# A mixture-of-experts kernel on one core: the last token block made, scaled and scattered in two halves of its channels

## The chip, the cores and the metric

The kernel runs on one core of one Trainium2 chip. The metric is the device time of one execution in microseconds (us), given as the median of several executions; lower is better. Engine names in the rows: PE is TensorE (matmuls), PEld is its weight load, DVE is VectorE, ACT is ScalarE, POOL is GpSimd, SP is SyncE, which issues most plain DMAs. The indirect DMAs, which gather or scatter rows by a list of row numbers, are issued by POOL.

## What is computed

The input x has 8 x 256 tokens of 512 channels in f32. A first layer adds a gated recurrent mix to x (an exponentially decaying average over time of a context, weighted by exp of the normalised x). A second layer adds a gated mixture of experts, and it is in this layer that the change lies:

```
logits = flat_x @ Wg + bg                       # 2048 tokens, 4 experts
top_vals, top_idx = top_k(logits, 2)            # each token picks 2 experts
for i in range(4):                              # experts
    sel_p, sel_idx = top_k(score_i, 512)        # each expert keeps its 512 best tokens
    tok = flat_x[sel_idx]                       # 512 x 512
    h = gelu(tok @ W1[i])                       # 512 x 2048
    y = h @ W2[i] * p                           # 512 x 512, one factor for each token
    out = out.at[sel_idx].add(y)
x = x + tanh(g_ffn) * out
```

## The kernel before

The first part of the program (about the first 130 us) computes the recurrent layer, stores x1 to the result tensor in HBM, stores its normalised rows to a table in HBM, and picks each expert's 512 tokens. Then the four experts follow one another. For an expert, POOL gathers the 512 token rows from the table in four blocks of 128, PE turns them over, and they are split into a high and a low f16 half, as are both weight matrices. A product in near-f32 precision is three f16 matmuls: high by high, high by low, low by high.

`up_product` makes h for one expert: 16 slices of 128 hidden units, each 12 matmuls with 512 tokens in the moving operand. ACT applies the gelu (line 954), DVE splits h in `halves_of_h_and_w2` (lines 1528 to 1533).

`down_block(e, s)` makes the output rows of token block s (128 tokens, of which an expert has ST = 4) for expert e: for each of HT = 16 slices of hidden units it loads the 128 tokens of h as the stationary operand and streams the 512 channels of W2, three times for the three halves, so 48 matmuls of 128x512. They accumulate in one PSUM bank, `PY[s % 2]`, bank 2 or 3. When it is done, PE raises `c_y`. DVE's `take_y(e, s)` (line 1548) multiplies the bank by the token's factor `yscale` into a buffer in SBUF, `y_c[:, s % 2]`, and raises `c_yout`; it first waits until the block that held this buffer before has been scattered (`c_add`). POOL's `scatter` (line 1107) then issues one indirect DMA that adds the 128 rows of 512 channels to the rows of the result in HBM whose numbers stand in `idx[:, e, s]`. The add is done by the DMA (`compute_op=ALU.add`), and raises `c_add[s % 2]` by 16 when it has landed. `down_block` waits for `c_yout` of the block before last, so that its bank is free.

The order of all this is written out by hand, per engine; semaphores alone tie the engines together. In experts 0 to 2 the scatter lies beside the next expert's work. In expert 3, the last, nothing follows: after the last `down_block`, `take_y` and the last scatter run one behind the other, and POOL then waits in `added` for all scatters to land, which ends the program.

Semaphores that begin at START = 4 are `c_y` and `c_yout`; E = 4 experts, D = 512 channels, P = 128.

Of the kernel before, what the change touches and what calls it, by code (L numbers as in the profile page):

```python
# [19 lines left out]
P = 128  # L20
BATCH, SEQ, D = 8, 256, 512
N = BATCH * SEQ
E, H, TOPK = 4, 2048, 2
# [3 lines left out]
HT = H // P  # L27
ST = CAP // P
# [16 lines left out]
START = 4  # L45
# [3 lines left out]
ALU = mybir.AluOpType  # L49
# [6 lines left out]
U32 = mybir.dt.uint32  # L56
# [65 lines left out]
def program(nc, x, ctx_in, w1, w2, scalars, consts, out):  # L122
    xn2_table = nc.dram_tensor("xn2_table", (N, D), F32, kind="Internal").ap()
    x_v = x.rearrange("b s d -> (b s) d").rearrange("(t p) d -> p t d", p=P)
    c_v = ctx_in.rearrange("b s d -> (b s) d").rearrange("(t p) d -> p t d", p=P)
    out_rows = out.rearrange("b s d -> (b s) d")
    out_v = out_rows.rearrange("(t p) d -> p t d", p=P)
    xn2_v = xn2_table.rearrange("(t p) d -> p t d", p=P)
    w1_v = w1.rearrange("e (k p) h -> p e k h", p=P)
# [3 lines left out]
    with stack:  # L133
        def sb(name, shape, dt=F32):
            return stack.enter_context(nc.sbuf_tensor(name, shape, dt))

        def sem(name):
            return stack.enter_context(nc.semaphore(name))
# [23 lines left out]
        def part(home, at, dims, dt=F32):  # L162
            cols = math.prod(dims)
            words = cols * (2 if dt in (F16, BF16) else 4) // 4
            v = home[:, at[0]:at[0] + words]
            at[0] += words
            v = v if dt == F32 else v.bitcast(dt)
            if len(dims) == 2:
                return v.rearrange("p (a b) -> p a b", a=dims[0])
            if len(dims) == 3:  # L170
                return v.rearrange("p (a b c) -> p a b c", a=dims[0], b=dims[1])
            return v
# [32 lines left out]
        w2_hi = part(arena, at, (HT, D), F16)  # L205
        w2_lo = part(arena, at, (HT, D), F16)
        h_hi = part(arena, at, (HT, CAP), F16)
        h_lo = part(arena, at, (HT, CAP), F16)
# [4 lines left out]
        y_c = part(arena, at, (2, D))  # L213
# [47 lines left out]
        rest = sb("rest", [P, E, TT])  # L261
        idx = sb("idx", [P, E, ST], U32)
        none = sb("none", [P, 1], U32)
        plist = sb("plist", [P, E, ST])

        wmax = sb("wmax", [P, 2, 2 * CT])
# [8 lines left out]
        yscale = sb("yscale", [P, ST])  # L275

        ps = stack.enter_context(nc.psum_tensor("ps", [P, 8, 512], F32))
        PX, PL = 4, 7
        PR = [5, 6] * (TT // 2 - 1) + [3, 0]
        PC, PW, PF, PG, PI = 7, 4, 5, 6, 4  # L280
        PT_L = 1
        PH, PY, PT, PT0 = [0, 1, 6, 7], [2, 3], [4, 5], [2, 3, 4, 5]


# [80 lines left out]
        b_taken = sem("list_taken")  # L365
# [25 lines left out]
        c_y = sem("y_in_psum")  # L391
        c_yscs = sem("yscale_steps")
        c_yout = sem("y_rows_ready")
        c_add = [sem("rows_added_0"), sem("rows_added_1")]

        def start(eng, *sems):
# [6 lines left out]
        def hold(eng, name):  # L403

            eng.sem_inc(passed[name], 1)
# [105 lines left out]
        def _(pe):  # L511
# [51 lines left out]
            def router_rows(part):  # L563

                pe.wait_ge(s_ltc, part + 1)
                for b in (2 * part, 2 * part + 1):
                    last = nc.tensor.transpose(ps[:, PT_L, b * P:(b + 1) * P], lgt[:, b * P:(b + 1) * P], ident)
                last.then_inc(s_ltt, 1)
# [6 lines left out]
            for k in range(CT):  # L575
                last = nc.tensor.matmul(ps[:, PL, 0:E], ones32[:, :], wg_raw[:, k, :], start=k == 0, stop=k == CT - 1)
# [25 lines left out]
            for i in range(TT // Q):  # L602
                if i % (TT // Q // 2) == 0:
                    pe.wait_ge(b_wide, i // (TT // Q // 2) + 1)
                last = nc.tensor.transpose(ps[:, 0, i * P:(i + 1) * P], prob_x[:, i, :], ident)
# [14 lines left out]
            for t in range(TT):  # L620
                if t % (TT // 2) == 0:
                    pe.wait_ge(b_hot, t // (TT // 2) + 1)
                last = nc.tensor.matmul(ps[:, PI, 0:ST * 4], hot[:, t, :], put[:, 0, t, :], start=t == 0, stop=t == TT - 1)
            last.then_inc(b_hotused, 1)

            def next_list(e):

                for t in range(TT):
                    if t % (TT // 2) == 0:
                        pe.wait_ge(b_hot, e * 2 + t // (TT // 2) + 3)  # L630
                    some = put[:, e + 1, t, :] if isinstance(e, int) else \
                        put[:, bass.ds(e + 1, 1), t, :].rearrange("p a c -> p (a c)")
                    last = nc.tensor.matmul(ps[:, PI, 0:ST * 4], hot[:, t, :], some,
                                            start=t == 0, stop=t == TT - 1)
                last.then_inc(b_hotused, 1)


            def tokens(done, blocks):

                for s in range(ST):  # L640
                    pe.wait_ge(c_tok[s], (done + 1) * 16)
                pe.wait_ge(b_taken, done * 2 + 2)
                for k in blocks:

                    if k >= 2:
                        pe.wait_ge(c_tokhi, START + done * CT + k - 1)
                        pe.wait_ge(c_toklo, START + done * CT + k - 1)
                    for s in range(ST):
                        last = nc.tensor.transpose(ps[:, PT[k % 2], s * P:(s + 1) * P], tok[:, s, k * P:(k + 1) * P], ident)  # L649
                    last.then_inc(c_tokt, 1)  # L650
# [71 lines left out]
            def down_block(e, s):  # L722

                pe.wait_ge(c_yout, START + e * ST + max(s - 1, 0))
                for t in range(HT):
                    if s == 0:
                        pe.wait_ge(c_hhi, START + e * HT + t + 1)
                        pe.wait_ge(c_hlo, START + e * HT + t + 1)
                        pe.wait_ge(c_w2hi, START + e * HT + t + 1)
                        pe.wait_ge(c_w2lo, START + e * HT + t + 1)  # L730
                    for n, (h, w) in enumerate(((h_hi, w2_hi), (h_hi, w2_lo), (h_lo, w2_hi))):
                        last = nc.tensor.matmul(ps[:, PY[s % 2], :], h[:, t, s * P:(s + 1) * P], w[:, t, :],  # L732
                                                start=t == 0 and n == 0, stop=t == HT - 1 and n == 2)
                last.then_inc(c_y, 1)

            def next_expert(e):

                next_list(e)
                down_block(e, 0)
                down_block(e, 1)  # L740
                tokens(e + 1, (0, 1))
                down_block(e, 2)
                tokens(e + 1, (2, 3))
                down_block(e, 3)

            first_tokens()
            first_group()
            up_product(0, 1)
            next_expert(0)
            with pe.Fori(1, E - 1) as e:  # L750
                up_product(e)
                next_expert(e)
            up_product(E - 1)
            for s in range(ST):
                down_block(E - 1, s)


        @block.scalar
# [231 lines left out]
        def _(pool):  # L990
# [111 lines left out]
            def scatter(e, tiles):  # L1102

                for s in tiles:
                    pool.wait_ge(c_yout, START + e * ST + s + 1)
                    hold(pool, "pool")
                    nc.gpsimd.indirect_dma_start(out_rows, bass.IndirectOffsetOnAxis(ap=idx[:, e, s:s + 1], axis=0),  # L1107
                                                 y_c[:, s % 2, :], None,
                                                 bounds_check=N - 1, compute_op=ALU.add).then_inc(c_add[s % 2], 16)

            def added(e):

                for n in range(2):
                    pool.wait_ge(c_add[n], (e + 1) * 16 * ST // 2)


            for g in range(NG):
# [5 lines left out]
                                         bounds_check=N - 1, compute_op=ALU.bypass).then_inc(c_none, 16)  # L1123
# [4 lines left out]
            for e in range(E - 1):  # L1128
# [4 lines left out]
                share_top(2 * e + 4, 1)  # L1133
                scatter(e, [3])
                added(e)
            scatter(E - 1, range(ST))
            added(E - 1)


        @block.vector  # L1140
        def _(dve):
# [164 lines left out]

            routed = ps[:, PT_L, :].rearrange("p (b q r) -> p q b r", b=CT, q=NG - 1)[:, :, :, 0:E]
            inner, edge = TT - SPT, CT - SPT
# [227 lines left out]
            def row_scale(e):  # L1536

                nc.vector.tensor_scalar(yscale[:, :], plist[:, e, :], tgate[:, 1:2], h_up[:, 0:1],
                                        ALU.mult, ALU.mult).then_inc(c_yscs, 1)
                dve.wait_ge(c_yscs, START + 2 * e + 1)  # L1540
                nc.vector.tensor_scalar(yscale[:, :], yscale[:, :], up[:, 1:2], None, ALU.mult).then_inc(c_yscs, 1)
                dve.wait_ge(c_yscs, START + 2 * e + 2)

            def take_y(e, s):
                dve.wait_ge(c_y, START + e * ST + s + 1)
                if e > 0 or s >= 2:
                    dve.wait_ge(c_add[s % 2], 16 * (e * (ST // 2) + s // 2))
                nc.vector.tensor_scalar(y_c[:, s % 2, :], ps[:, PY[s % 2], :], yscale[:, s:s + 1], None, ALU.mult).then_inc(c_yout, 1)  # L1548
# [32 lines left out]
            dve.wait_ge(c_y, START + (E - 1) * ST)  # L1581
            halves_of_h_and_w2(E - 1, 0, HT // HB)
            row_scale(E - 1)
            for s in range(ST):
                take_y(E - 1, s)


_INS = ["x", "ctx_2048", "L0_ffn_W1", "L0_ffn_W2"]
# [33 lines left out]
```

## Time and profile before

| what | value |
|---|---|
| time, median of 3 executions | 487.35 us (486.91 to 487.68) |
| time of the profiled execution | 487.14 us |
| its span, first to last instruction | 485.3 us |
| mean granted TensorE clock, as a share of full speed | 0.952 |
| PE busy | 414.9 us (85% of the span) |
| DVE, ACT, POOL busy | 313.8, 263.7, 106.2 us |

The profiled execution's time is 1.84 us more than its span; this part lies outside the first and the last instruction. Times inside the trace count from the span's start. A group row gives the busy time in us and the mean ns of one instruction. Matmuls overlap one another, so their mean duration is longer than the distance from one to the next.

### The profile page before, as it was taken

The numbers are of one execution on the slowest core, as the hardware profiler recorded it, in microseconds if no ns is written. First come the engines' busy times: TensorE is split into PE (matmuls) and PEld (weight loads), VectorE is DVE, ScalarE is ACT, GpSimd is POOL, SyncE is SP. The second block draws the span as 40 slices with busy tenths as digits, with TensorE's granted clock in tenths as the row PEclk, the third lists the DMA queues.
The fourth block names the chain that finished last, engine by engine and source line by source line (L and its number), as shares of the span: only waits on it lengthen the run. The fifth ranks groups of instructions, "written<-read, shape, count | busy, mean of one in ns | idle before, by whom it ended". The sixth has DMA issues, their size and how long they took to land.

```text
span 485.3 us, 7222 instructions
## 1 busy us (share of the span) xinstructions
PE 414.9 (85%) x2032; PEld 200.9 (41%) x2032; DVE 313.8 (65%) x601; ACT 263.7 (54%) x411; POOL 106.2 (22%) x122
## 2 busy tenths in 40 slices
PE   2586877710399999999999999999999999999992
PEld 2343343310174444444444444444444444444440
DVE  7999999988659994374797156379715637770000
ACT  6578888998227546942554793254479325440000
POOL 0777756601120004121000502100050210001111
PEclk9999998955599999999999999999999999999997
DMA  7894120599025307557000926600092310000211
GB/s 258 334 360 161 43 88 1 187 345 355 22 66 198 150 0 279 176 155 257 0 1 15 384 59 211 200 0 0 14 382 58 43 23 0 0 0 5 40 23 22
DMA packets 23126, 59.62 MB, mean 123 GB/s; under 512 B 1280, under 2 KB 1408, under 8 KB 21056
## 3 DMA queue, kind: packets, MB, share of 16 engines
q1 hardware_dynamic: 19008, 50.15, 27.7%
q0 software_dynamic: 3664, 8.65, 8.6%
q10 hardware_dynamic: 432, 0.54, 0.3%
q8 instruction: 11, 0.18, 0.2%
q14 instruction: 11, 0.09, 0.0%
HBM read 46.76 MB, written 12.58 MB: 122 GB/s over the span
## 4 chain that ended last, share of the span: by engine, by line
PE 73%; DVE 19%; issue 4%; ACT 1%; POOL 1%; DMA 1%; DVEq 0%; POOLq 0%
PE ps L732 34%; PE ps L717 32%; DVE arena L1164 6%; DVE arena L1183 2%; PE ps L678 2%; DVE arena L1194 2%; DVE arena L1422 2%; DVE bn L1149 1%; PE ps L649 1%; PE ps L655 1%; DMA small<-in_scalars 1%; DVE arena L1477 0%; DVE arena L1171 0%; PE ps L670 0%; PE ps L609 0%
## 5 line engine op out<-in xcount | busy, mean ns | idle before, releaser
L732 PE MATMUL ps<-arena 128*128 128x512 f16 x768 | 167.4, 379 | 0.0
L717 PE MATMUL ps<-arena,early 128*128 128x512 f16 x720 | 156.1, 379 | 0.0
L732 PEld LDWEIGHTS ps<-arena 128*128 128x128 f16 x768 | 74.9, 98 | 88.6
L717 PEld LDWEIGHTS ps<-arena,early 128*128 x720 | 70.5, 98 | 84.9
L954 ACT ACTIVATE arena<-ps,up 128x512 f32<-128x512 f32 x64 | 44.0, 687 | 82.1 <-PE ps L717 74.4
L1548 DVE TENSOR_SCALAR arena<-ps,yscale 128x512 f32<-128x512 f32 x16 | 12.0, 750 | 77.7 <-PE ps L732 57.4
L949 ACT ACTIVATE arena<-rows,down x64 | 45.6, 712 | 30.1 <-PE ps L732 30.1
L1107 POOL DMA_INDIRECT result<-arena,idx x16 | 26.0, 1625 | 158.2 <-DVE arena L1548 156.7
L1533 DVE SCALAR_TENSOR_TENSOR arena<-arena,h_down 128x512 f32 x64 | 48.1, 752 | 9.6 <-DVE arena L1531 0.8
L1508 DVE SCALAR_TENSOR_TENSOR early<-w_raw,down,early 128x2048 f16<-128x2048 f32 x16 | 36.8, 2345 | 22.3 <-ACT early L912 22.3
L1528 DVE SCALAR_TENSOR_TENSOR arena<-rows,down,arena x64 | 47.8, 747 | 1.6 <-ACT arena L949 1.5
L1098 POOL DMA_INDIRECT arena<-xn_table,idx x16 | 16.8, 1049 | 140.8 <-DVE plist L1491 137.1
L1531 DVE TENSOR_SCALAR arena<-arena,h_down 128x512 f32 x64 | 31.0, 484 | 23.9 <-ACT arena L954 23.9
L1164 DVE TENSOR_TENSOR_SCAN arena<-arena,ps 128x1024 f32<-128x1024 f32 (+1 forms) x20 | 37.1, 1853 | 0.0
L522 PE MATMUL ps<-cst,early 128*128 128x128 f32 x64 | 13.6, 325 | 27.1 <-DVE arena L1179 11.9
L912 ACT ACTIVATE early<-w_raw,down 128x2048 f16<-128x2048 f32 x16 | 30.7, 1989 | 7.2 <-DVE down L1368 7.2
L933 ACT ACTIVATE arena<-rows 128x2048 bf16<-128x2048 f32 x16 | 30.4, 1906 | 1.2 <-DMA rows<-in_L_ffn_W 1.2
L920 ACT ACTIVATE arena<-w_raw 128x2048 bf16<-128x2048 f32 x12 | 22.8, 1898 | 8.3 <-DVE arena L1533 8.3
L1040 POOL TENSOR_TENSOR arena<-arena 128x512 f32<-128x512 f32 (+1 forms) x19 | 20.4, 1073 | 17.9 <-ACT arena L847 17.4
L522 PEld LDWEIGHTS ps<-cst,early 128*128 128x128 f32 x64 | 7.9, 157 | 34.9 <-DVE arena L1179 17.3
L560 PE MATMUL ps<-arena,wg_c 128*4 128x512 f32 (+1 forms) x40 | 19.1, 564 | 0.0
L844 ACT ACTIVATE arena<-arena,chan 128x512 f32<-128x512 f32 (+1 forms) x20 | 12.7, 633 | 10.7 <-DVE arena L1179 10.6
(184 smaller groups left out, 386.9 us busy)
## 6 DMA issues: line engine op xcount, KB each, us to landing
w_raw<-in_L_ffn_W SPq DMA_DIRECT2D x4, 4096.0 KB, 13.7
rows<-in_L_ffn_W SPq DMA_DIRECT2D x3, 4096.0 KB, 16.5
rows<-in_L_ffn_W SPq DMA_DIRECT2D x4, 1024.0 KB, 11.2
result<-rows SPq DMA_DIRECT2D x3, 1024.0 KB, 6.8
early<-in_ctx SPq DMA_DIRECT2D x2, 1024.0 KB, 6.6
rows<-in_x SPq DMA_DIRECT2D x2, 1024.0 KB, 11.6
xn_table<-arena SPq DMA_DIRECT2D x4, 512.0 KB, 5.4
xn_table<-arena SPq DMA_DIRECT2D x2, 1024.0 KB, 5.9
```

What stands on the lines that cost most here:

```text
L717: last = nc.tensor.matmul(ps[:, PH[q], :], w[:, k, at], t[:, k, :], start=n == 0, stop=n == 3 * CT - 1)
L732: last = nc.tensor.matmul(ps[:, PY[s % 2], :], h[:, t, s * P:(s + 1) * P], w[:, t, :], start=t == 0 and n == 0, stop=t == HT - 1 and n == 2)
L912: nc.scalar.activation(w1_hi[:, k, :], w1_raw[:, k, :], ACT.Copy, scale=down[:, 0:1]).then_inc(c_w1hi, 1)
L933: nc.scalar.activation(spent[:, k % 2, :], some, ACT.Abs, scale=1.0 / (HT * D // CT), accum_out=wmax[:, 1, k:k + 1]).then_inc(c_w2sum, 1)
L949: nc.scalar.activation(w2_hi[:, bass.ds(at, 1), :].rearrange("p a d -> p (a d)"), w2_raw[:, bass.ds(at, 1), :].rearrange("p a d -> p (a d) ...
L954: nc.scalar.activation(h_f[:, q, :], ps[:, PH[q], :], ACT.Gelu, scale=up[:, 0:1]).then_inc(c_gelu, 1)
L1107: nc.gpsimd.indirect_dma_start(out_rows, bass.IndirectOffsetOnAxis(ap=idx[:, e, s:s + 1], axis=0), y_c[:, s % 2, :], None, bounds_check=N ...
L1164: nc.vector.tensor_tensor_scan(state[:, u % 2, 1:size + 1], decay[:, u % CT, 0:size], pair(u, 0, size), 0.0, ALU.mult, ALU.add).then_inc(s ...
L1508: nc.vector.scalar_tensor_tensor(w1_lo[:, :, some], w1_raw[:, :, some], down[:, 0:1], w1_hi[:, :, some], ALU.mult, ALU.subtract).then_inc( ...
L1528: nc.vector.scalar_tensor_tensor(row(w2_lo), row(w2_raw), down[:, 1:2], row(w2_hi), ALU.mult, ALU.subtract).then_inc(c_w2lo, 1)
L1531: nc.vector.tensor_scalar(row(h_hi), h_f[:, q, :], h_down[:, 0:1], None, ALU.mult).then_inc(c_hhi, 1)
L1533: nc.vector.scalar_tensor_tensor(row(h_lo), h_f[:, q, :], h_down[:, 0:1], row(h_hi), ALU.mult, ALU.subtract).then_inc(c_hlo, 1)
```

## The change

Only the last block (s = 3) of the last expert (e = 3) is treated differently. PE makes its 128 rows in two halves of 256 channels: `last_halves` issues 48 matmuls of 128x256 for channels 0 to 255 into bank 3, raises `c_y`, then 48 for channels 256 to 511 into bank 0, and raises `c_y` again. DVE scales each half as it comes. POOL issues an indirect DMA for each half. For that the result is viewed as 4096 rows of 256 channels (`out_halves`), and DVE writes the numbers 2 * idx and 2 * idx + 1 into a new small tensor, `idx_half`, ahead of its first `take_y` of this expert. Each half has its own semaphore `c_last[n]`, and POOL waits at the end for both of them, and for the other scatters.

```diff
+    out_halves = out.rearrange("b s (a d) -> (b s a) d", a=2)
...
+        idx_half = sb("idx_half", [P, 2], U32)
...
-        PT_L = 1
+        PT_L, LAST = 1, (3, 0)
...
+            def last_halves():
+
+                for n in range(2):
+                    cols = slice(n * D // 2, (n + 1) * D // 2)
+                    pe.wait_ge(c_yout, START + (E - 1) * ST + (ST - 2))
+                    for t in range(HT):
+                        for i, (h, w) in enumerate(((h_hi, w2_hi), (h_hi, w2_lo), (h_lo, w2_hi))):
+                            last = nc.tensor.matmul(ps[:, LAST[n], 0:D // 2], h[:, t, (ST - 1) * P:ST * P], w[:, t, cols],
+                                                    start=t == 0 and i == 0, stop=t == HT - 1 and i == 2)
+                    last.then_inc(c_y, 1)
...
-            for s in range(ST):
+            for s in range(ST - 1):
                 down_block(E - 1, s)
+            last_halves()
...
-            scatter(E - 1, range(ST))
-            added(E - 1)
+            scatter(E - 1, range(ST - 1))
+            pool.wait_ge(c_half, 2)
+            for n in range(2):
+                cols = slice(n * D // 2, (n + 1) * D // 2)
+                pool.wait_ge(c_yout, START + (E - 1) * ST + ST + n)
+                hold(pool, "pool")
+                nc.gpsimd.indirect_dma_start(out_halves, bass.IndirectOffsetOnAxis(ap=idx_half[:, n:n + 1], axis=0),
+                                             y_c[:, (ST - 1) % 2, cols], None,
+                                             bounds_check=2 * N - 1, compute_op=ALU.add).then_inc(c_last[n], 16)
+            pool.wait_ge(c_add[0], E * 16 * ST // 2)
+            pool.wait_ge(c_add[1], (E * ST // 2 - 1) * 16)
+            pool.wait_ge(c_last[0], 16)
+            pool.wait_ge(c_last[1], 16)
...
-            for s in range(ST):
+            for n in range(2):
+                dve.wait_ge(b_taken, 2 * E)
+                nc.vector.tensor_scalar(idx_half[:, n:n + 1], idx[:, E - 1, ST - 1:ST], 1, n,
+                                        ALU.logical_shift_left, ALU.bitwise_or).then_inc(c_half, 1)
+            for s in range(ST - 1):
                 take_y(E - 1, s)
+            dve.wait_ge(c_add[1], 16 * ((E - 1) * (ST // 2) + 1))
+            for n in range(2):
+                cols = slice(n * D // 2, (n + 1) * D // 2)
+                dve.wait_ge(c_y, START + (E - 1) * ST + ST + n)
+                nc.vector.tensor_scalar(y_c[:, (ST - 1) % 2, cols], ps[:, LAST[n], 0:D // 2], yscale[:, ST - 1:ST], None,
+                                        ALU.mult).then_inc(c_yout, 1)
```

On PE, the end of the program before, from block 2 of the last expert on. `ps` is the PSUM, `arena` the SBUF region that holds h and W2, and `y_rows_ready` is the semaphore `c_yout`:

```order
L732 MATMUL ps<-arena 128x512 [waits y_rows_ready]
L732 MATMUL ps<-arena 128x512 x47
L732 MATMUL ps<-arena 128x512 [waits y_rows_ready]
L732 MATMUL ps<-arena 128x512 x47
L133 UNCONDITIONAL_BRANCH
```

and the same place of the change:

```order
L736 MATMUL ps<-arena 128x512 [waits y_rows_ready]
L736 MATMUL ps<-arena 128x512 x47
L747 MATMUL ps<-arena 128x256 [waits y_rows_ready]
L747 MATMUL ps<-arena 128x256 x47
L747 MATMUL ps<-arena 128x256 [waits y_rows_ready]
L747 MATMUL ps<-arena 128x256 x47
L134 UNCONDITIONAL_BRANCH
```

The last 48 matmuls of 512 columns have become 96 of 256 columns; nothing else on PE has moved.

On DVE, the end of the program before, from the row factors of the last expert on. `rows_added_0` and `rows_added_1` are `c_add`, `y_in_psum` is `c_y`:

```order
L1538 TENSOR_SCALAR yscale<-plist,tgate,h_up 128x4
L1541 TENSOR_SCALAR yscale<-yscale,up 128x4 [waits yscale_steps]
L1548 TENSOR_SCALAR arena<-ps,yscale 128x512 [waits rows_added_0,y_in_psum,yscale_steps]
L1548 TENSOR_SCALAR arena<-ps,yscale 128x512 [waits rows_added_1,y_in_psum]
L1548 TENSOR_SCALAR arena<-ps,yscale 128x512 [waits rows_added_0,y_in_psum]
L1548 TENSOR_SCALAR arena<-ps,yscale 128x512 [waits rows_added_1,y_in_psum]
L133 UNCONDITIONAL_BRANCH
```

and of the change:

```order
L1565 TENSOR_SCALAR yscale<-plist,tgate,h_up 128x4
L1568 TENSOR_SCALAR yscale<-yscale,up 128x4 [waits yscale_steps]
L1613 TENSOR_SCALAR idx_half<-idx 128x1 [waits list_taken,yscale_steps]
L1613 TENSOR_SCALAR idx_half<-idx 128x1 [waits list_taken]
L1575 TENSOR_SCALAR arena<-ps,yscale 128x512 [waits rows_added_0,y_in_psum]
L1575 TENSOR_SCALAR arena<-ps,yscale 128x512 [waits rows_added_1,y_in_psum]
L1575 TENSOR_SCALAR arena<-ps,yscale 128x512 [waits rows_added_0,y_in_psum]
L1621 TENSOR_SCALAR arena<-ps,yscale 128x256 [waits y_in_psum,rows_added_1]
L1621 TENSOR_SCALAR arena<-ps,yscale 128x256 [waits y_in_psum]
L134 UNCONDITIONAL_BRANCH
```

Two instructions of one column have come in ahead of the first scaling, and the last scaling of 512 columns has become two of 256.

On POOL, the end of the program before, from the third expert's scatters on. `result` is the output tensor, `idx` the row numbers:

```order
L1107 DMA result<-arena,idx 2048x512 [waits y_rows_ready] x3
L1091 ISA wall<-wtop 128x1 [waits weight_top_ready,weight_power_ready]
L1107 DMA result<-arena,idx 2048x512 [waits y_rows_ready]
L1107 DMA result<-arena,idx 2048x512 [waits y_rows_ready,rows_added_0,rows_added_1]
L1107 DMA result<-arena,idx 2048x512 [waits y_rows_ready] x3
L133 UNCONDITIONAL_BRANCH [waits rows_added_1,rows_added_0]
```

and of the change, from the last expert's first scatter on:

```order
L1123 DMA result<-arena,idx 2048x512 [waits y_rows_ready,rows_added_0,rows_added_1]
L1123 DMA result<-arena,idx 2048x512 [waits y_rows_ready] x2
L1158 DMA result<-arena,idx_half 4096x256 [waits half_rows_numbered,y_rows_ready]
L1158 DMA result<-arena,idx_half 4096x256 [waits y_rows_ready]
L134 UNCONDITIONAL_BRANCH [waits last_rows_added_0,last_rows_added_1,rows_added_1,rows_added_0]
```

The last scatter of 128 rows of 512 channels has become two of 128 rows of 256 channels each, and the end of the program waits for four semaphores in place of two.

## Rows read from the trace of the kernel before

**Rows 1.** The chain that ended last, 430 to 486 us: start, length, what.

```profile
434.27 41.45 PE ps L732 x192
475.73 0.03 issue
475.75 0.76 DVE arena L1548
476.51 0.02 issue
...
476.65 0.72 issue
477.37 1.55 POOL result L1107
```

**Rows 2.** Windows of a quarter microsecond behind it: length, PE, PEld, DVE, ACT, POOL, clock, DMA share, GB/s.

```profile
479.00:479.25 0.25, 0.00 (x0) 0.00 (x0) 0.00 (x0) 0.00 (x0) 0.00 (x0) 1.00 0.00 0
479.25:479.50 0.25, 0.00 (x0) 0.00 (x0) 0.00 (x0) 0.00 (x0) 0.00 (x0) 1.00 0.10 8
...
481.50:481.75 0.25, 0.00 (x0) 0.00 (x0) 0.00 (x0) 0.00 (x0) 0.00 (x0) 0.50 0.07 8
481.75:482.00 0.25, 0.00 (x0) 0.00 (x0) 0.00 (x0) 0.00 (x0) 0.00 (x0) 0.50 0.00 0
```

**Rows 3.** Matmul forms over the whole span, and the weight loads of 136 to 149 us.

```profile
L732 PE MATMUL ps<-arena 128*128 128x512 f16 x768 | 167.4, 379 | 0.0
...
L678 PE MATMUL ps<-arena,early 128*128 128x256 f16 x64 | 7.3, 272 | 0.5 <-ACT arena L976 0.5
...
L678 PE MATMUL ps<-arena,early 128*128 128x512 f16 x16 | 3.6, 379 | 0.0
...
L678 PEld LDWEIGHTS ps<-arena,early 128*128 128x128 f16 x80 | 7.8, 98 | 3.1 <-issue 0.8
```

**Rows 4.** Timeline of PE, 136 to 149 us: start, length, what.

```profile
136.63 1.91 PE L678 MATMUL ps<-arena,early 128*128 128x256 f16 x16 [0.55 <-ACT arena L976]
138.37 1.04 PE L670 MATMUL ps<-cst,arena 128*128 128x128 f32 x8
139.24 8.86 PE L678 MATMUL ps<-arena,early 128*128 128x256 f16 x64
147.94 1.24 PE L717 MATMUL ps<-arena,early 128*128 128x512 f16 x5
```

**Rows 5.** Windows of line 678 alone: length, PE, PEld, clock, DMA share, GB/s.

```profile
139.30:144.00 4.70, 4.70 (x44) 4.21 (x44) 1.00 0.00 0
```

**Rows 6.** Forms of DVE over the whole span.

```profile
L1548 DVE TENSOR_SCALAR arena<-ps,yscale 128x512 f32<-128x512 f32 x16 | 12.0, 750 | 77.7 <-PE ps L732 57.4 <-issue 20.3
...
L1183 DVE SCALAR_TENSOR_TENSOR arena<-arena,chan,ps 128x512 f32<-128x512 f32 x12 | 8.9, 740 | 0.0
...
L1183 DVE SCALAR_TENSOR_TENSOR arena<-arena,chan,ps 128x256 f32<-128x256 f32 x8 | 3.8, 475 | 0.0
...
L1443 DVE TENSOR_TENSOR cand<-digit,nxt 128x1 int32<-128x1 int32 x8 | 1.3, 159 | 0.3
```

**Rows 7.** The last expert's scalings and scatters in the timeline, 439 to 486 us.

```profile
444.73 0.75 DVE L1548 TENSOR_SCALAR arena<-ps,yscale 128x512 f32<-128x512 f32 x1 [7.66 <-PE ps L732]
...
455.03 0.75 DVE L1548 TENSOR_SCALAR arena<-ps,yscale 128x512 f32<-128x512 f32 x1 [9.55 <-PE ps L732]
456.65 1.55 POOL L1107 DMA_INDIRECT result<-arena,idx  x1 [8.64 <-DVE arena L1548]
465.39 0.75 DVE L1548 TENSOR_SCALAR arena<-ps,yscale 128x512 f32<-128x512 f32 x1 [9.61 <-PE ps L732]
467.00 1.55 POOL L1107 DMA_INDIRECT result<-arena,idx  x1 [8.81 <-DVE arena L1548]
```

**Rows 8.** Lines 1107 and 1098 (scatters, gathers): min, median, max of POOL's instruction.

```profile
L1107 POOL DMA_INDIRECT result<-arena,idx x16: 1550/1568/1843, 193.8 to 477.4; - x16
...
L1098 POOL DMA_INDIRECT arena<-xn_table,idx x16: 1011/1018/1277, 130.6 to 356.7; - x16
```

**Rows 9.** Windows over the last scatter's data, and over the last but one's.

```profile
479.25:481.75 2.50, 0.00 (x0) 0.00 (x0) 0.00 (x0) 0.00 (x0) 0.00 (x0) 0.63 0.80 105
469.00:471.25 2.25, 2.25 (x13) 1.00 (x11) 0.00 (x0) 0.00 (x0) 0.00 (x0) 1.00 0.86 117
```

**Rows 10.** DMA queues of 130 to 139 us (4 gathers), then of 476 to 486 us (1 scatter).

```profile
q0 software_dynamic: 320, 1.05, 40.4%
...
q0 software_dynamic: 144, 0.26, 20.0%
```

More of the change, by code:

```diff
@@ L393, in program @@
         c_yout = sem("y_rows_ready")
+        c_half = sem("half_rows_numbered")
+        c_last = [sem("last_rows_added_0"), sem("last_rows_added_1")]
         c_add = [sem("rows_added_0"), sem("rows_added_1")]
```

## The prediction

> **What bounds the kernel now.** I read the chain that ended last first, since the change touches only its last pieces. It says that PE runs the 192 matmuls of the last expert's four blocks without a gap, 41.45 us, to 475.73; then DVE scales the last block (0.76 us), 0.86 us pass before POOL's indirect DMA starts (477.37), and that instruction takes 1.55 us, to 478.92 [rows 1]. The chain stops there, so the windows behind it come next: the data of the last scatter move from about 479.4 to about 481.6, and after 481.75 no DMA moves [rows 2]. The span ends at 485.3, so some 3.6 us more pass until the add is confirmed and the program closes. From PE's end to the span's end is thus 9.6 us in which no other work runs. PE's stage itself is the bound before that. The reader is to see that only three pieces of this tail have a size that 256 channels in place of 512 can touch: the scaling, POOL's instruction, and the data.
>
> **PE: 48 matmuls become 96.** Of 512 columns, one every 41.45 / 192 = 0.2159 us [rows 1], so the block takes 48 x 0.2159 = 10.36 us. For 256 columns of f16 there is a stage of before: line 678 streams 256 columns with another 128x128 weight load for each, like the changed block. The run that begins at 139.24 holds 64 matmuls, and the next line begins at 147.94 [rows 4]. Of the 64, 16 are of 512 columns [rows 3]; 16 of the 64 with 256 columns stand in the earlier run at 136.63, so 48 are left here. Then 8.70 - 16 x 0.2159 = 5.25 us for 48, or 0.1093 us each. The changed block takes 96 x 0.1093 = 10.49 us: **+0.13 us**. The clock in that stage was granted in full (1.00, the level of 2.4 GHz) [rows 5], as it was in the last stage [rows 9]. What makes this close: the loads are 98 ns each [rows 3] and fill 4.21 of 4.70 us [rows 5], so they fit under 109 ns with little to spare. In the last stage DVE and ACT are nearly idle, so nothing disturbs them more than there. The two waits of `last_halves` are for block 1's scaling, which is over at 455.8 [rows 7], ten us before the first half starts; bank 3's last reader was that same scaling, and bank 0's a gelu before 434. They cost nothing.
>
> **The first half** is off the path. It is in PSUM at 465.4 + 48 x 0.1093 + about 0.2 = 470.8, is scaled by 471.3, its POOL instruction runs from about 472.2 to 473.7, and its data move from about 474.2 for at most the 2.3 us of a whole block, to 476.5. The data of the scatter of block 2 are through at 471.25 [rows 9], and POOL's instruction for it (467.00 to 468.55) is long over. The second half needs POOL at 476.4 and the DMA engines at 479, so both are free: margins of 2.7 and 2.5 us. DVE's wait for the scatter of block 1 (issued 456.65, [rows 7]) was met some ten us before.
>
> **The row numbers.** Two DVE instructions of one column, about 159 ns each by an integer one of that size [rows 6], in front of block 0's scaling. DVE stood idle 7.66 us there [rows 7], so they cost nothing; without that cover it would be 0.3 us. POOL's wait for them is met 30 us early.
>
> **DVE's last scaling: 512 to 256 columns from PSUM.** No such TENSOR_SCALAR of 256 is there. Another f32 operation of DVE with an operand in PSUM goes from 740 to 475 ns [rows 6], 265 ns less; from 750 I take 485. **-0.27 us**, with bounds of 0.20 and 0.37 (half of it all).
>
> **POOL's last instruction.** It makes descriptors for 128 rows, before and after, and their count doesn't change. The rows show 1550 to 1843 ns for scatters and 1011 ns at the least for gathers of as many rows [rows 8], so the type matters, and I have no row that varies the bytes. I take **0**, since the last four scatters all take 1.55; the bounds are -0.54 (as quick as a gather) and +0.29 (the slowest scatter). The 0.86 us ahead of it (0.72 of it issue) is the same for every scatter.
>
> **The data of the last scatter.** Before: 0.80 of 2.50 us, 2.00 us for each of the 16 engines [rows 9], for 8 rows of 2 KB each, so 0.25 us a row. A gather of such rows, without the add, takes 40.4% of 9 us for four, 0.91 us each [rows 10], 0.11 us a row. The bounds for half the bytes are 0 (a row costs what it costs) and half of it all, -1.0. I take the plain moving part as going with bytes and the extra of the add as a cost for each row: half of 0.91, **-0.45 us**. This value is chosen, not shown. The Trainium skill, page "DMA: Bandwidth & Descriptors", section "Anatomy of one DMA — SWDGE (gpsimd) path", gives a DMA about 2.0 us fixed plus its bytes over 436 GB/s, most of the fixed part being the receipt of the write. By it 131 KB less would be an estimated 0.30 us less, and the whole sum -0.44 instead of -0.59; the 3.6 us between the last data and the end agree with a large part that bytes don't touch.
>
> **The sum.** +0.13 - 0.27 + 0 - 0.45 = **-0.59 us** against the profiled execution's 487.14 (485.3 of span and 1.84 around it): 486.55. That execution was 0.21 under the median of its runs, so for the median I say 487.35 - 0.59 = **486.8 us**, 0.12% less. What a measurement of this kernel can tell from no change is about 0.2%, 0.97 us (its three runs spread over 0.77 us). All ends together: 0.13 - 0.37 - 0.54 - 1.0 = -1.78 at the best and 0.13 - 0.20 + 0.29 + 0 = +0.22 at the worst, so 485.6 to 487.6.
>
> **The rivals.**
> - **Everything behind PE goes with bytes.** The data halve (-1.0), DVE gives 0.27, PE takes 0.13: -1.14, 486.2; with POOL also as quick as a gather -1.68, 485.7. For it: a gathered row costs less than half of an added one, so the add may be work for each byte too. Against it: the count of rows and descriptors stays. Chance 0.20, faster.
> - **The transfer does not shrink.** Then only the scaling is won: -0.14, 487.2, within 0.2%. The change would make a first half early that nobody waits for. For it: the row's cost of 0.25 us is more than twice that of a plain one of the same bytes, so it may be a round trip. Chance 0.25, no change.
> - **My forecast**, the sum above: chance 0.45, no change.
> - **A weight load that shows (slower).** Each of the 48 added matmuls brings a load of 98 ns [rows 3]. If the loads don't hide behind 256 columns here, all of them laid bare would be 48 x 0.098 = +4.7, so 491.5 with my other terms; it decides from +1.56 us on (0.97 and the 0.59 that the rest gives back), which is 16 ns on each of the 96, a spacing of 125 ns in place of 109. Against it: [rows 3 to 5] show 48 in a row at 109 with a fresh load each. For it: a slack of 11 ns only, and the instructions come twice as fast as in the rest of the stage. Chance 0.07.
> - **A dearer close.** Three more semaphores and two more waits lie in the 3.6 us behind the data or in the 1.84 us outside the span; of neither does a row show the parts. A microsecond and a half would make it slower, 488.3. Nothing in the rows speaks for so much. Chance 0.03.
>
> The Trainium skill, page "TensorE: Matmul & The Clock Gate", section "Back-to-back issue gap", has a rule by which the load rival would come true: in a stream of load and matmul pairs the spacing is set by both, 81 ns for 128 columns and 131 ns for 512. That is an estimated 64 ns for each matmul and 0.13 for each column, and 48 more matmuls would cost 3.1 us. This case's trace disagrees: 215.9 ns at 512 columns and 109.3 at 256 leave 2.7 ns for each matmul, which is why the rival gets no more.
>
> **How the numbers follow.** Faster by over 0.2%: 0.20. Within 0.2%: 0.25 + 0.45 = 0.70. Slower: 0.07 + 0.03 = 0.10. The range leaves out the slow cases and the far end of the fast one (POOL as quick as a gather): from 486.0 to 487.8, the upper end being the worst sum of the terms and 0.2 for the spread of the runs. It holds both no-change cases and most of the fast one.
>
> **What the profile after would show.** Line 747: 96 matmuls in about 10.5 us, with no gap between the halves; PE ends 0.13 us later after its last expert's start. Line 1621: two instructions of about 485 ns, the second right behind PE's end. Line 1158: two of about 1.55 us, the first ending some 3.5 us before the second starts. In quarter windows the last data last about 1.7 us in place of 2.2. I am wrong if line 747 takes over 11 us, if the last data last under 1.3 us or over 2.1 us, if POOL's instruction goes with bytes, or if the time from the last data to the end moves.

## The result

The changed kernel takes 486.12 us (median of 16 executions, 485.81 to 486.69) where the kernel before takes 487.19 us (median of 16, 486.67 to 487.68): 1.07 us less, a ratio of 0.9977 with a 95% interval of 0.9970 to 0.9984. A second comparison gave 486.13 against 487.10, 0.9978 (0.9969 to 0.9987). That is inside the range of the prediction and 0.7 us under its point. The kernel became a little faster: a ratio of 1 lies outside the interval. Whether the gain is past the 0.2% that I had set as the line of no change is not settled, since it measured 0.22% and then 0.20%.

The profiled execution took 486.11 us with a span of 484.3. Its chain that ended last, from the last token blocks on (start, length, what), answers to [rows 1]:

```profile
434.31 31.08 PE ps L736 x144
465.39 10.49 PE ps L747 x96
475.88 0.02 issue
475.90 0.50 DVE arena L1621
...
476.53 0.51 issue
477.05 0.02 POOLq L1163
477.06 0.19 issue
477.25 1.55 POOL result L1158
```

PE's 96 matmuls of 256 columns take 10.49 us, to the hundredth what was predicted, and 0.13 more than the 48 of 512. The scaling is 0.50 instead of 0.76 us. POOL's instruction is as long as before. Counted from the start of the last block, POOL's last instruction begins after 477.25 - 465.39 = 11.86 us; before it was 477.37 - (475.73 - 10.36) = 12.00 us. So 0.14 us of the 1.07 is won ahead of it, and the rest must lie behind it.

The timeline of the same stretch, which answers to [rows 7], shows the first half out of the way:

```profile
465.42 0.75 DVE L1575 TENSOR_SCALAR arena<-ps,yscale 128x512 f32<-128x512 f32 x1 [9.61 <-PE ps L736]
467.04 1.55 POOL L1123 DMA_INDIRECT result<-arena,idx  x1 [8.81 <-DVE arena L1575]
470.74 0.48 DVE L1621 TENSOR_SCALAR arena<-ps,yscale 128x256 f32<-128x256 f32 x1 [4.56 <-PE ps L747]
472.08 1.55 POOL L1158 DMA_INDIRECT result<-arena,idx_half  x1 [3.48 <-issue]
475.90 0.48 DVE L1621 TENSOR_SCALAR arena<-ps,yscale 128x256 f32<-128x256 f32 x1 [4.68 <-PE ps L747]
477.25 1.55 POOL L1158 DMA_INDIRECT result<-arena,idx_half  x1 [3.63 <-DVE arena L1621]
```

POOL had been idle 3.63 us when the second half came. The windows behind it, in quarters of a microsecond (length, busy engines, clock, DMA share, GB/s), answer to [rows 2, 9]:

```profile
479.00:479.25 0.25, 0.00 (x0) 0.00 (x0) 0.00 (x0) 0.00 (x0) 0.00 (x0) 0.50 0.00 0
479.25:479.50 0.25, 0.00 (x0) 0.00 (x0) 0.00 (x0) 0.00 (x0) 0.00 (x0) 0.50 0.92 57
479.50:479.75 0.25, 0.00 (x0) 0.00 (x0) 0.00 (x0) 0.00 (x0) 0.00 (x0) 0.50 0.65 82
479.75:480.00 0.25, 0.00 (x0) 0.00 (x0) 0.00 (x0) 0.00 (x0) 0.00 (x0) 0.50 1.19 160
480.00:480.25 0.25, 0.00 (x0) 0.00 (x0) 0.00 (x0) 0.00 (x0) 0.00 (x0) 0.50 1.12 176
480.25:480.50 0.25, 0.00 (x0) 0.00 (x0) 0.00 (x0) 0.00 (x0) 0.00 (x0) 0.50 0.35 45
480.50:480.75 0.25, 0.00 (x0) 0.00 (x0) 0.00 (x0) 0.00 (x0) 0.00 (x0) 0.50 0.03 4
480.75:481.00 0.25, 0.00 (x0) 0.00 (x0) 0.00 (x0) 0.00 (x0) 0.00 (x0) 0.50 0.00 0
```

and over the whole of it, in the window that [rows 9] has for before:

```profile
479.25:481.75 2.50, 0.00 (x0) 0.00 (x0) 0.00 (x0) 0.00 (x0) 0.00 (x0) 0.50 0.43 52
```

The last data begin to move about where they did and are through some 1.0 us earlier: they last from about 479.3 to 480.5, some 1.2 us, against 2.2 before. The packets take 0.43 x 2.50 = 1.07 us on each of the 16 engines, against 0.80 x 2.50 = 2.00 us in [rows 9], for the same 8 rows each at half the bytes. (The DMA share sums the time of packets, and in short windows it can be over 1, as it is in two quarters here; it is no strict busy time.) The profile's median from the issue of a scatter to its landing says the same in one number, the last of this row (before 4.7; for the second half alone 3.7 too):

```profile
result<-arena,idx_half POOLq DMA_INDIRECT x2, 3.7
```

From that start to the end of the span there were 485.3 - 477.37 = 7.9 us before, and there are 484.3 - 477.25 = 7.1 now; what follows the landing is 3.2 and 3.4 us, which the change did not shorten.

### The profile page after: what moved, and what is told of

It reads as the page before. It is cut to its first block, busy times and chain, and to the rows that moved or that the text cites. A ratio compares the mean times of both kernels' runs of the same rounds, so it can differ in the third digit from the quotient of the medians.

```text
span 484.3 us, 7326 instructions
## 1 busy us (share of the span) xinstructions
PE 413.8 (85%) x2080; PEld 204.8 (42%) x2080; DVE 314.0 (65%) x604; ACT 263.5 (54%) x411; POOL 108.3 (22%) x123
## 4 chain that ended last, share of the span: by engine, by line
PE 72%; DVE 20%; issue 4%; DMA 1%; ACT 1%; POOL 1%; DVEq 0%; POOLq 0%
PE ps L736 32%; PE ps L721 32%; DVE arena L1191 7%; DVE arena L1210 2%; PE ps L682 2%; PE ps L747 2%; DVE arena L1221 2%; DVE arena L1449 2%; DVE bn L1176 1%; PE ps L653 1%; DMA arena<-xn_table,idx 1%; DMA small<-in_scalars 1%; DVE arena L1198 1%; DVE arena L1504 0%; PE ps L613 0%
## 5 line engine op out<-in xcount | busy, mean ns | idle before, releaser
L736 PE MATMUL ps<-arena 128*128 128x512 f16 x720 | 157.0, 379 | 0.0
L736 PEld LDWEIGHTS ps<-arena 128*128 128x128 f16 x720 | 70.2, 98 | 82.9
L1123 POOL DMA_INDIRECT result<-arena,idx x15 | 24.4, 1630 | 149.4 <-DVE arena L1575 147.9
L1056 POOL TENSOR_TENSOR arena<-arena 128x512 f32<-128x512 f32 (+1 forms) x19 | 20.4, 1071 | 17.7 <-ACT arena L863 17.2
```

## The experiments

Each was timed beside the kernel before on the same chip: e1 to e4 on one, e5 to e8 on a second, e9 and e10 on a third. My theory after the result was that the cost of a row in the adding DMA goes with its bytes (theory "bytes"), so that the gain is the shorter last transfer; the rival was that the rows cost what they cost and the gain came from elsewhere (theory "rows").

**e1: only the scatter in two.** PE and DVE as before; the last scatter is two DMAs of 256 channels.

```diff
-            scatter(E - 1, range(ST))
+            scatter(E - 1, range(ST - 1))
+            for n in range(2):
+                pool.wait_ge(c_yout, START + E * ST)
+                nc.gpsimd.indirect_dma_start(out_halves, ...idx_half[:, n:n + 1]..., y_c[:, (ST - 1) % 2, cols], ...)
```

> PE and DVE as in the kernel before (one block of 512 columns, one scaling), only the last scatter is two DMAs of 256 channels, issued one behind the other. Theory 'bytes' (a row's cost in the DMA goes with its bytes): POOL's second instruction ends 1.55 + 0.3 = 1.85 us later than the only one before, but the data behind it are half, about 1.0 us less: +0.85 us against before, landing of each about 3.7 us. Rival 'rows' (a row costs what it costs; the gain of the change lies elsewhere): +1.85 us, landing 4.7 us.

Measured: 488.07 against 487.07 us, ratio 1.0019 (1.0010 to 1.0028), +1.00 us, near the +0.85 of "bytes". The timeline has both instructions:

```profile
477.59 1.55 POOL L1146 DMA_INDIRECT result<-arena,idx_half  x1 [8.80 <-DVE arena L1563]
479.44 1.55 POOL L1146 DMA_INDIRECT result<-arena,idx_half  x1 [0.30 <-issue]
```

The second begins 1.85 us after the first, and the landing of 3.8 us gives 0.9 of it back. "Rows" would have had +1.85. POOL's instruction takes 1.55 us for rows of 1 KB as it did for rows of 2 KB, so a split alone loses: it must be paid for under PE's work.

**e2: PE and DVE in two, one scatter.**

```diff
-            for n in range(2):
-                pool.wait_ge(c_yout, START + (E - 1) * ST + ST + n)
-                nc.gpsimd.indirect_dma_start(out_halves, ...idx_half[:, n:n + 1]..., y_c[:, (ST - 1) % 2, cols], ...)
+            pool.wait_ge(c_yout, START + (E - 1) * ST + ST + 1)
+            nc.gpsimd.indirect_dma_start(out_rows, ...idx[:, E - 1, ST - 1:ST]..., y_c[:, (ST - 1) % 2, :], ...)
```

> PE and DVE in two halves as in the change, but one scatter of 512 channels when both are scaled. Theory 'bytes': only +0.13 (96 matmuls) and -0.27 (scaling) are left, so -0.14 us against before, no measurable change, and the last data take 2.0 us per engine as before. Rival (the gain comes from PE or DVE, or from an end that is quicker by itself): about -1.1 us, as the whole change.

Measured: 487.05 against 487.07 us, ratio 0.9999 (0.9990 to 1.0008). The gain is gone, though PE and DVE do all that the change makes them do. Its last data, in the window of [rows 9], and its queue over the 12 us of 476 to 488:

```profile
479.25:481.75 2.50, 0.00 (x0) 0.00 (x0) 0.00 (x0) 0.00 (x0) 0.00 (x0) 0.50 0.77 99
...
q0 software_dynamic: 144, 0.26, 17.7%
```

0.77 of 2.50 us is 1.9 us for each engine, but the data begin a little before this window; 17.7% of 12 us is 2.12 us, against 2.00 before, and the landing is 4.8 us. e1 and e2 together place the gain: it needs the early first half and the short last transfer, and comes through the transfer.

**e3: half of the last half sent.** A third point of bytes, at 512 B a row. The kernel leaves out channels 384 to 511 of the last block, so it is a probe and no version to use. The cut shows only the DMA; the row numbers of the second scatter are those of the view in quarters.

```diff
-                nc.gpsimd.indirect_dma_start(out_halves, ... y_c[:, (ST - 1) % 2, cols], ...)
+                sent = cols if n == 0 else slice(D // 2, 3 * D // 4)
+                nc.gpsimd.indirect_dma_start((out_halves, out_quarters)[n], ... y_c[:, (ST - 1) % 2, sent], ...)
```

> The change, but of the last half's 256 scaled channels only 128 are scattered (rows of 512 B; channels 384 to 511 of the last block are left out). Theory 'bytes': from 2.00 us at 2 KB and 1.07 us at 1 KB per engine, a line with 0.13 fixed and 0.93 for each KB gives 0.60 us, so -0.47 against the change and about -1.55 us against before. Rival 'floor' (below 1 KB the count of rows sets the time): data stay at about 1.0 us, -1.1 us against before. POOL's instruction 1.55 us by both.

Measured: 485.66 against 487.07 us, ratio 0.9970 (0.9958 to 0.9982), -1.41 us. Landing of the last scatter, and its queue over 12 us (packets, MB, share of 16 engines), of this kernel:

```profile
q0 software_dynamic: 144, 0.07, 6.3%
...
result<-arena,idx_half POOLq DMA_INDIRECT x1, 3.3
```

and the queue of the changed kernel in the same window:

```profile
q0 software_dynamic: 144, 0.13, 8.9%
```

6.3% of 12 us is 0.76 us an engine, 8.9% is 1.07. There is no floor at 1 KB, but the line is not straight: 2 KB rows take 2.00 us, 1 KB 1.07 and 512 B 0.76, so 0.93 for the second KB and 0.31 for the half before it. I had expected 0.60 us and a time 1.55 us under before.

**e4: no add.** The last block's two scatters overwrite, so the kernel leaves out the add of this block: a probe as well.

```diff
-                                             bounds_check=2 * N - 1, compute_op=ALU.add).then_inc(c_last[n], 16)
+                                             bounds_check=2 * N - 1, compute_op=ALU.bypass).then_inc(c_last[n], 16)
```

> The change, but the two scatters of the last block overwrite the rows instead of adding to them (the add of the last block is left out). Theory 'the add is work on each byte, and extra descriptors for POOL': POOL's instruction 1.0 us as for the gathers instead of 1.55, data about 0.5 us per engine instead of 1.07, so about -1.1 us against the change and -2.2 us against before. Rival 'the add is free, writing to HBM is what costs': POOL perhaps shorter but the data stay at 1.07 us, -0.5 us against the change at the most, -1.6 us against before.

Measured: 484.95 against 487.07 us, ratio 0.9953 (0.9939 to 0.9967), -2.12 us. POOL's instruction in the chain, and the queue over 12 us:

```profile
477.38 1.02 POOL result L1158
```

```profile
q0 software_dynamic: 48, 0.13, 3.1%
...
result<-arena,idx_half POOLq DMA_INDIRECT x1, 2.5
```

The same bytes to the same rows take 3.1% of 12 us, 0.37 us an engine, against 1.07 with the add, and 48 packets against 144. So the add is most of the data's cost, and 0.53 us of POOL's instruction. What in it costs so much (the read of the old rows, the add itself, or the smaller packets) this run does not separate. It shows what a better version has to do.

**e5: the changed kernel again**, beside e6 to e8 on one chip.

> The changed kernel itself, beside the next three on one chip: about -1.1 us against before, as in its first comparison.

Measured: 486.13 against 487.10 us, ratio 0.9978 (0.9969 to 0.9987), -0.97 us.

**e6: the add on DVE.** POOL gathers the block's rows of the result ahead of the last expert's scatters, when all earlier experts have been added and no other block of this expert touches them. DVE's scaling becomes scale and add, and the scatter is plain.

```diff
+            nc.gpsimd.indirect_dma_start(tok[:, 0, :], None, out_rows, ...idx[:, E - 1, ST - 1:ST]..., compute_op=ALU.bypass)
             scatter(E - 1, range(ST - 1))
...
-                nc.vector.tensor_scalar(y_c[:, (ST - 1) % 2, cols], ps[:, LAST[n], 0:D // 2], yscale[:, ST - 1:ST], None,
-                                        ALU.mult).then_inc(c_yout, 1)
+                nc.vector.scalar_tensor_tensor(y_c[:, (ST - 1) % 2, cols], ps[:, LAST[n], 0:D // 2], yscale[:, ST - 1:ST],
+                                               tok[:, 0, cols], ALU.mult, ALU.add).then_inc(c_yout, 1)
```

> The change, but the add of the last block is taken out of the DMA: ahead of the last expert's scatters POOL gathers the block's present rows of the result into SBUF, DVE's scaling of each half becomes scale and add in one instruction (475 ns for 256 columns in the rows of another such operation, as the scaling), and both scatters write without adding. Theory from the run without the add: POOL's instruction 1.02 instead of 1.55, landing 2.5 instead of 3.7 us, nothing more on DVE, so about -2.1 us against before and -1.0 against the change, with the full result. Rival: the gather in front of the last expert's scatters, or DVE's third operand, costs something on the path, then -1.6 us or less against before.

Measured: 485.03 against 487.10 us, ratio 0.9955 (0.9942 to 0.9969), -2.07 us, with the full result computed: as much as the run without the add gave. DVE and POOL in the timeline:

```profile
476.30 0.48 DVE L1627 SCALAR_TENSOR_TENSOR arena<-ps,yscale,arena 128x256 f32<-128x256 f32 x1 [4.66 <-PE ps L748]
477.68 1.01 POOL L1163 DMA_INDIRECT result<-arena,idx_half  x1 [4.12 <-DVE arena L1627]
```

The add costs DVE nothing: scale and add take the same 0.48 us as the scaling alone. POOL's instruction for as many rows takes 1.01 instead of 1.55 us. The gather is off the path: POOL starts it at 401.10 and has nothing to issue from there to 446.72.

**e7: the same in one piece.** PE, DVE and scatter of the last block whole again, with e6's add on DVE.

```diff
-            last_halves()
+            down_block(E - 1, ST - 1)
...
+            nc.vector.scalar_tensor_tensor(y_c[:, (ST - 1) % 2, :], ps[:, PY[(ST - 1) % 2], :], yscale[:, ST - 1:ST],
+                                           tok[:, 0, :], ALU.mult, ALU.add).then_inc(c_yout, 1)
```

> The same move of the add, but the last block is in one piece again (one group of 48 matmuls of 512 columns, one scale and add of 512, one plain scatter of 2 KB rows). Theory: PE gives back 0.13, DVE takes 0.26 more, and the plain data of 256 KB take some 0.4 to 0.5 us more than those of 128 KB, so -1.5 us against before, about 0.6 us more than in halves. Rival: a plain row costs the same at 1 and at 2 KB, then only 0.13 us more than in halves, -2.0 us against before.

Measured: 485.47 against 487.10 us, ratio 0.9960 (0.9947 to 0.9974), -1.63 us. Its queue over 476 to 488 us and its landing:

```profile
q0 software_dynamic: 80, 0.26, 5.7%
...
result<-arena,idx POOLq DMA_INDIRECT x1, 2.8
```

Moving the add is by itself worth more than the split (-1.63 us against the -0.97 of e5 on the same chip). The plain 2 KB rows take 5.7% of 12 us, 0.68 us an engine, where the adding ones took 2.00. With plain rows half the bytes save only 0.3 us (2.8 to 2.5 to the landing, 0.68 to 0.37 on an engine), where they save 1.0 with the add. The Trainium skill, page "DMA: Bandwidth & Descriptors", section "Anatomy of one DMA — SWDGE (gpsimd) path", fits the time of a DMA as 2.0 us and its bytes over 436 GB/s, by which 131 KB less save an estimated 0.30 us. These two runs agree with it, and the adding DMA, with its 1.0 us, does not.

**e8: 384 channels, then 128.**

```diff
-        PT_L, LAST = 1, (3, 0)
+        PT_L, LAST, SPLIT = 1, (3, 0), (0, 3 * D // 4, D)
```

The first piece is scattered as 256 and 128 channels (two DMAs, one by the view in halves and one by the view in quarters), the last as 128.

> The change with another split: 384 channels first (48 matmuls of 384 columns, scattered as 256 and 128 channels), then 128 channels (48 matmuls of 128 columns). Behind PE it should give 0.13 (scaling) and 0.4 us (data of 512 B rows) against the change. Theory 'loads bind': 48 matmuls of 384 at 0.163 us are 7.8 us, and those of 128 columns can't come faster than their weight loads of 98 ns, so 4.7 us or more; PE then takes 2.0 us more than in the change, and the whole is +1.5 us against the change and about +0.5 against before. Rival 'a matmul costs its columns alone' (0.416 ns for each column and 2.7 ns): 56 ns for 128 columns, PE as in the change, -0.5 us against the change and -1.6 against before.

Measured: 486.97 against 487.10 us, ratio 0.9996 (0.9987 to 1.0005). Neither side had it. The timeline:

```profile
473.45 0.62 DVE L1623 TENSOR_SCALAR arena<-ps,yscale 128x384 f32<-128x384 f32 x1 [7.12 <-PE ps L748]
474.93 1.55 POOL L1159 DMA_INDIRECT result<-arena,idx_half  x1 [6.18 <-DVE arena L1623]
476.25 0.35 DVE L1623 TENSOR_SCALAR arena<-ps,yscale 128x128 f32<-128x128 f32 x1 [2.18 <-PE ps L748]
476.79 1.55 POOL L1159 DMA_INDIRECT result<-arena,idx_half  x1 [0.30 <-DVE arena L1623]
478.64 1.55 POOL L1159 DMA_INDIRECT result<-arena,idx_half  x1 [0.30 <-issue]
```

The second group of 48 matmuls took 476.25 - 473.45 = 2.80 us, 58 ns each: the loads of 98 ns don't bind, and my theory on them is wrong. But POOL is late: the first piece is scaled only at 474.07, its two DMAs keep POOL until 478.34, and the third, whose data are scaled at 476.60, has to wait. Counted from the start of the last block it begins after 13.09 us, 1.2 us later than in the change, and that eats what the small last piece gives back. A queue on POOL is a rival that I had not named.

**e9: three pieces, 256, 128 and 128 channels**, one DMA each, so that POOL has time between them.

```diff
-        PT_L, LAST = 1, (3, 0)
+        PT_L, LAST, SPLIT = 1, (3, 0, 1), (0, D // 2, 3 * D // 4, D)
```

> The last block in three pieces of 256, 128 and 128 channels, each scattered by one adding DMA, so that POOL has time between them and only rows of 512 B lie behind PE. From the uneven split, 48 matmuls of 128 columns take 2.80 us: PE takes 5.25 + 5.60 = 10.85 us, 0.36 more than in halves. Behind it: 0.13 less for the scaling and 0.4 less to the landing. Theory: -0.17 us against the change, about -1.25 against before, hardly to be told from the change. Rival: POOL's instruction for the second piece is not over when the third is ready (by my count it ends at 476.2 and the third wants it at 476.9, span time), then it is slower than the change.

Measured: 485.46 against 487.10 us, ratio 0.9967 (0.9955 to 0.9979), -1.64 us. The chain and the landing:

```profile
464.82 10.62 PE ps L748 x144
475.44 0.02 issue
475.46 0.36 DVE arena L1623
...
476.68 1.55 POOL result L1159
```

```profile
result<-arena,idx_half POOLq DMA_INDIRECT x1, 3.2
```

144 matmuls take 10.62 us, 0.13 more than 96, and not 0.36: they follow the columns (48 x 0.1093 + 96 x 0.056). That is most of why the gain is more than the 1.25 us expected. POOL was free 1.13 us before the third piece, so the rival did not come. With the landing 1.5 us shorter than before this adds up to the measured time.

**e10: three pieces and the add on DVE**, e9 with the edit of e6.

> The same three pieces, with the add on DVE and plain scatters. Theory: PE 0.36 more than in halves, scaling 0.13 less, and of the plain data only some 0.1 to 0.15 us less, so +0.1 us against the halves with the add on DVE, about -2.0 against before: halves stay the best split there. Rival: what follows PE shrinks as much as with the adding DMA (0.4), then -0.17 us, -2.2 against before.

Measured: 484.79 against 487.10 us, ratio 0.9953 (0.9940 to 0.9967), -2.31 us, the lowest time of all, with the full result computed. Both sides expected less (-2.0 and -2.2): the third piece cost PE 0.12 us and not 0.36, and the landing fell to 2.2 us. From e6 it differs by 0.24 us across two chips and with overlapping intervals, so whether the third piece pays there isn't settled.

Two terms, each read from a profile, give nearly all of it: how long after the start of the last block POOL's last instruction begins (before: 12.00), and how long from there to the landing (before: 4.7).

| kernel | POOL's last begins after | landing | sum against before | measured |
|---|---|---|---|---|
| the change | 11.86 | 3.7 | -1.14 | -1.07 |
| e1 two DMAs only | about 13.85 | 3.8 | +0.95 | +1.00 |
| e2 one scatter | 11.86 | 4.8 | -0.04 | -0.02 |
| e3 512 B rows | 11.87 | 3.3 | -1.53 | -1.41 |
| e4 no add | 11.90 | 2.5 | -2.30 | -2.12 |
| e6 add on DVE | 11.90 | 2.5 | -2.30 | -2.07 |
| e7 add on DVE, whole | about 12.12 | 2.8 | -1.78 | -1.63 |
| e8 uneven | 13.09 | 3.3 | -0.31 | -0.13 |
| e9 three pieces | 11.86 | 3.2 | -1.64 | -1.64 |
| e10 three, add on DVE | 11.87 | 2.2 | -2.63 | -2.31 |

The sums are up to 0.3 us more than what was measured. The landings are single profiled executions and are given to 0.1 us. The sums also leave out what follows the landing: by the same profiles 3.2 us to the end of the span before, and 3.3 to 3.6 in the others, with the 3.6 in e10, where the sum misses most. Why it grows, no run shows.

## Why the prediction came out as it did

The time lies in the range, 0.12 us above its lower end, but the case that I held most likely did not come: the range holds the result because it was drawn wide enough for a rival. Of the 0.68 us between the point and the result, 0.48 are gain that I had not forecast (1.07 in place of 0.59). Most of the rest is that the kernel before had a median of 487.19 us in 16 executions, where it had 487.35 in 3. Term by term:

- **What bounds the end** was right: nothing but the tail behind PE could change, and of it the scaling and the last data did.
- **PE, +0.13 us**: 10.49 us predicted and found. The reading of the 48 matmuls of line 678 as the price of 256 columns held.
- **The first half off the path**: held. Its scaling ended at 471.2 and its POOL instruction ran from 472.08 to 473.63, as computed, and POOL was idle 3.63 us before the second.
- **The row numbers, 0**: held; they are done at 437.3, and DVE then waits 7.36 us for block 0.
- **The scaling, -0.27**: 0.48 us found for 0.485 predicted.
- **POOL's last instruction, 0**: held, 1552 ns for both halves. The bound of -0.54 belonged to something else: e4 and e6 show that it is the add that makes 1.55 out of 1.02, and e3 and e7 that the bytes of a row do not.
- **The data, -0.45: this is the term that was mis-sized.** It measured -0.93 us of packet time on each engine, and -1.0 to the landing, which is the end "half of it all" of its range. I had split a row's cost into a plain part that goes with bytes and an extra of the add that is a cost for each row. The plain part was near: a plain scatter takes 0.68 us with 2 KB rows (e7) and 0.37 with 1 KB (e4), 0.31 less. The extra of the add was the mistake: it is 2.00 - 0.68 = 1.32 us at 2 KB and 1.07 - 0.37 = 0.70 at 1 KB, so it gave 0.62 us where I had put nothing. Only at 512 B, with 0.76 us where a quarter of 2.00 would be 0.50 (e3), does a part show clearly that does not go with the bytes. My own sign of being wrong came as well: the last data lasted some 1.2 us, under the 1.3 that I had named. So the rival "everything behind PE goes with bytes", with POOL unchanged, -1.14 us and 486.2, was the true case, and I had given it 0.20. The step from "a gathered row costs half" to "the difference is for each row" had no row behind it, and the prediction said so; the fault is that such a choice moved the weight to no change.
- **The weight load that shows**: the rival did not come, and e8 and e9 show that its slack was misread. I had put the 98 ns of a load beside the 109 ns of a matmul and found 11 ns left. Loads overlap one another as matmuls do: 128 columns go at 56 to 58 ns with a fresh load of 98 ns each. The Trainium skill, page "TensorE: Matmul & The Clock Gate", section "Back-to-back issue gap", also has a formula, columns over 2.4 plus 2.5 ns, which it gives for a single matmul without its load. By it 128 columns take 55.8 ns, 256 take 109.2 and 512 take 215.8. The traces, all with a load for each matmul, agree with it at all three (56 to 58, 109.3, 215.9); with the 81 and 131 ns that the section gives for pairs they don't.
- **The dearer close**: from the landing to the end 3.2 us before and 3.4 after, so three more semaphores and two more waits cost some 0.2 us at most in these two executions. The part outside the span stayed at 1.8 us.

## What to carry to other kernels

When a kernel ends in a chain of matmuls, a scaling and a scatter, cut the last piece so that only a small part is left to scale and to send, and pay for the extra DMA instruction under the matmuls: PE's price was 0.13 us for each further cut, while a cut of the DMA alone costs 1.85 us of POOL's time. Price a moved transfer by its own kind: an adding scatter and a plain one of the same rows differed by 1.9 us to the landing with 2 KB rows and by 1.2 with 1 KB, so an add that the vector engine can do in its scaling at no cost should leave the DMA. That is allowed only where nothing else writes those rows between the gather and the scatter, as for the last block here. And before a piece is made smaller, look at whether the engine that issues the DMAs is free again when the piece is ready.

## What was not expected of the hardware

- The adding scatter of 128 rows took 2.00, 1.07 and 0.76 us of each DMA engine for rows of 2 KB, 1 KB and 512 B, in 144 packets each time: one for a row, by the count, and 16 small ones. The plain scatter took 0.68 us in 80 packets for rows of 2 KB and 0.37 us in 48 for rows of 1 KB, which by the count is 4 KB to a packet.
- POOL's instruction for 128 rows took 1.55 us with the add, for rows of 512 B, 1 KB and 2 KB, and 1.01 to 1.04 without it, for rows of 1 KB and 2 KB (e4, e6, e7).
- PE's matmuls of 128 columns, each with a fresh 128x128 f16 load of 98 ns, followed one another at 56 to 58 ns.
